# One Trainium2 core: an operand order and placement change in a selective scan between two dense stages

## The chip, the cores and the metric

The kernel runs on one core of one Trainium2 chip. The metric is the device time of one execution in microseconds (us). Before the change three runs took 1060.62, 1064.67 and 1065.10 us, median 1064.67.

## The reference

The input x is (8, 256, 32, 32) in float32: 8 images, 256 channels, N = 1024 tokens. One block is computed, cut here to what matters:

```python
x = x + conv(ln_c(x))                      # ln over channels
t = to_tokens(x)
t = t + ffn(ln_t(t))                       # 8 experts, dense, weights from a thresholded softmax
# conv:
xz = silu(in_proj_w @ x + b)               # 768 x 256
x_ssm, res, gate = split(xz, 3)
xf = silu(depthwise_conv3(x_ssm))
dbc = dbc_w @ xf + b                       # per head: dt, B (8), C (8)
dt = softplus(dbc[:, :, 0])
# x_h, dt, B, C are gathered by perm, an argsort of a Moebius-mapped score (one per head)
h = exp(dt * A) * h + dt * B * x_t         # 8 states, 1024 steps, 2 heads of 128 channels
y_t = C . h + D * x_t
y = y gathered by the inverse of perm
y = y * silu(gate) + res
return silu(out_proj_w @ y + b)
```

## The kernel before, in words

There are three stages, and five engines that each run their own hand-written instruction list; semaphores are the only order between engines. A wait blocks all that stands behind it in that engine's list.

**Stage 1** (`batch(b)`, b = 0 to 7 on every engine) does one image per step: transposes and layer norm, the projection in 6 row blocks (`in_proj`, L1064, three-part products of a high and a low half), the convolution, `dbc` (L1074), and rows by token (`rows_by_tokens`). SyncE stores rows, res and gate to HBM. VectorE ranks the scores in batches 1 to 4 (`ranks`), turns ranks into places in batch 4 (`places`), and GpSimd scatters token numbers to `order_scratch` in batches 5 and 6 (`scatter_order`, 8 indirect DMAs each). SyncE loads the order (`turn`) in its part of batch 7. GpSimd then gathers the first chunks (`gather_rows`).

**Stage 2**, the scan (`body(q)`, q = 0 to 15), takes chunks of 64 tokens, all heads and 4 images in one chunk, so that 8 chunks make 1024 tokens for 4 images, and then the other 4 images follow. A chunk is computed as a kernel matrix and a state. On each engine one `body(q)` works on chunk q and on parts of q - 1, q + 1, q + 2 and q + 3:

- TensorE: `rows_of(q+1)` (transposes of B and C to bank 4), `products(q, ...)`, 8 matmuls C.B, one per state, cycling through banks 1, 2 and 3 (L1185), `times_of(q+1)` (dt summed up to each token, bank 5, L1122 and L1124), `y_of(q-1, 0)` and `y_of(q-1, 1)` (L1194, L1197, banks 6 and 7), `sums_of(q+2)` (L1102, bank 0), `states(q+1)` (L1135) and `columns(q+1)` (L1142).
- ScalarE: `decays` (8 exponentials of 128x512 into `ee`, which is tile `rg`, L921), `rows_high`, `block_decays`, `y_rows` (PSUM to SBUF, L927), `states_by_tile` (8 scaled copies to `hx`, L937), `columns` (L868).
- VectorE: `times_decay(q, s)` (ee times product, L1701), `whole_kernel(q-1)` (last sum, writes `kbd`, L1713), `rows_low`, `distances` (L1652), `weigh` (L1677, L1681), `flatten`, `exponents` (L1638, L1644), `next_states`.
- GpSimd: `add_state(q, s)` for s = 0 to 6 (running sum `ksum` in tile `sm`, L708), `up_to_token(q+2)` (dt times a triangle to `dtri`, L679), `gather_rows(q+3)` (L669).
- SyncE: `spread(q+1)` sends rows to HBM (L449) and reads them back in block form to `cr` and `bl` (L454, L456), which `products(q+1)` needs; then the store of y.

`decays(q, s)` waits until `add_state(q-1, s)` has read the same part of `ee`. `add_state(q, 0)` waits until `whole_kernel(q-1)` has read `ksum`:

```python
if s == 0:
    pool.wait_ge(dskip_ready, 2)
    pool.wait_ge(k_ready.sem, k_ready.at(c.q, 0))
```

**Stage 3** (`step3`, 16 steps of 512 tokens) gathers y, gates it, applies the out projection (L1255), adds the residual, layer norm by token, softmax gate, 8 experts (L1322, the bulk of TensorE's time). A step also prepares the front of the next one. The front of the very first step (gate, out projection, norm, logits) has no step to hide behind: it runs after chunk 15, with y gathered in part during chunks 13 to 15 (`gather_first`), and res and gate of the first half loaded in chunk 14 (`rg0`).

## Time and profile before

| What | Value |
|---|---|
| runs | 1060.62, 1064.67, 1065.10 us |
| the profiled execution | 1064.97 us |
| its span (first to last instruction) | 1063.2 us |
| busy: TensorE, VectorE, ScalarE, GpSimd | 930.4, 771.3, 508.6, 505.9 us |
| granted TensorE clock, mean | 0.917 of full |

The profile is of the one execution of 1064.97 us. The span leaves out 1.8 us before the first and after the last instruction. Busy time is an average over three stages with different limits, so it is read stage by stage.

### The profile page before, as it was taken

What the parts mean: (1) busy time and instruction counts of PE and PEld (TensorE: products, weight loads), DVE (VectorE), ACT (ScalarE), POOL (GpSimd) and SP (SyncE); (2) the same over time, 40 slices, a digit from 0 to 9 for tenths busy, and PEclk for the clock granted to TensorE, in tenths of its full rate; (3) what the DMA queues carried; (4) which work ended last, traced back from release to release, by engine and by line L of the source; (5) the groups of instructions that cost most, each with busy time, mean ns of one, the idle gap of its engine ahead of it and who ended that gap; (6) DMA issues with size and microseconds to landing.
All of it is one profiled execution on the core that took longest, in us unless ns stands there. A gap on an engine that the chain in (4) does not pass through costs nothing.

```text
span 1063.2 us, 15454 instructions
## 1 busy us (share of the span) xinstructions
PE 930.4 (88%) x4658; PEld 718.6 (68%) x4658; DVE 771.3 (73%) x2001; ACT 508.6 (48%) x924; POOL 505.9 (48%) x563
## 2 busy tenths in 40 slices
PE   4999999986687678666499999999999999999997
PEld 3887888874454445444367777777777777877776
DVE  5768887534677778775458787787787877878775
ACT  2777877664666665666223333332333323333330
POOL 2066666775887877788650333313333132330000
PEclk8999999996777887778689999999999999999999
DMA  5335674476254343334331131401314013140001
GB/s 162 119 89 171 190 191 147 116 175 177 76 144 126 98 120 109 117 108 156 126 133 44 33 145 39 147 30 39 138 39 158 21 38 138 39 158 20 20 1 39
DMA packets 63687, 110.05 MB, mean 104 GB/s; under 512 B 18538, under 2 KB 44436, under 8 KB 60564
## 3 DMA queue, kind: packets, MB, share of 16 engines
q1 hardware_dynamic: 56468, 91.41, 27.4%
q0 software_dynamic: 7168, 18.03, 5.9%
q8 instruction: 22, 0.36, 0.1%
q14 instruction: 29, 0.24, 0.1%
HBM read 61.51 MB, written 47.92 MB: 103 GB/s over the span
## 4 chain that ended last, share of the span: by engine, by line
PE 69%; DVE 7%; ACT 7%; issue 5%; POOL 5%; DMA 4%; ACTq 0%; SPq 0%; DVEq 0%; another core or an unknown queue 0%; POOLq 0%
PE bank L1322 31%; PE bank L1064 8%; PE bank L1230 4%; PE bank L1255 4%; PE bank L1185 3%; ACT xf L937 3%; PE bank L1283 2%; PE bank L1074 2%; PE bank L1194 2%; POOL sm L708 2%; PE bank L1197 2%; PE bank L1122 2%; PE bank L1092 2%; DMA score_scratch<-score 1%; PE bank L1267 1%
## 5 line engine op out<-in xcount | busy, mean ns | idle before, releaser
L763 POOL TENSOR_TENSOR ssm<-ssm,rg 128x512 f32<-128x512 f32 x30 | 35.2, 1192 | 269.7 <-DVE ssm L1799 269.7
L751 POOL DMA_INDIRECT xtm<-y_scratch,idxu x120 | 119.2, 993 | 68.6 <-issue 34.2
L1322 PE MATMUL bank<-wexph,xhl 128*128 128x512 f32 x512 | 144.9, 405 | 0.1
L1322 PE MATMUL bank<-wexph,cr 128*128 128x512 f32 x512 | 143.4, 401 | 0.1
L708 POOL TENSOR_TENSOR sm<-sm,rg 128x512 f32<-128x512 f32 x96 | 122.4, 1275 | 30.0 <-DVE rg L1701 20.1
L1701 DVE TENSOR_TENSOR rg<-rg,bank 128x512 f32<-128x512 f32 x128 | 83.2, 681 | 60.6 <-ACT rg L921 39.9
L1322 PEld LDWEIGHTS bank<-wexph,xhl 128*128 128x128 f32 x512 | 93.8, 189 | 23.4 <-DVE xf L1903 2.0
L1322 PEld LDWEIGHTS bank<-wexph,cr 128*128 128x128 f32 x512 | 93.4, 189 | 22.0 <-DVE ysb L1903 1.7
L921 ACT ACTIVATE rg<-dists,aown 128x512 f32<-128x512 f32 x128 | 84.7, 714 | 0.0
L1322 PE MATMUL bank<-wexpl,xhl 128*128 128x512 f32 x256 | 80.6, 396 | 0.0
L1322 PE MATMUL bank<-wexpl,cr 128*128 128x512 f32 x256 | 80.3, 395 | 0.0
L1898 DVE SCALAR_TENSOR_TENSOR ysb<-bank,soft,ysb 128x256 f32<-128x256 f32 x128 | 58.3, 479 | 25.1 <-PE bank L1322 23.0
L1898 DVE SCALAR_TENSOR_TENSOR xf<-bank,soft,xf 128x256 f32<-128x256 f32 x128 | 57.8, 479 | 24.4 <-PE bank L1322 21.5
L1064 PE MATMUL bank<-xhl,winh 128*128 128x512 f32 x192 | 55.0, 408 | 4.0 <-ACT ssm L813 2.0
L1064 PE MATMUL bank<-cr,winh 128*128 128x512 f32 x192 | 55.5, 412 | 3.1 <-ACT ssm L813 2.8
L1322 PEld LDWEIGHTS bank<-wexpl,xhl 128*128 128x128 f32 x256 | 48.3, 189 | 11.6
L1322 PEld LDWEIGHTS bank<-wexpl,cr 128*128 128x128 f32 x256 | 48.1, 188 | 11.3
L1903 DVE SCALAR_TENSOR_TENSOR xf<-bank,soft,xf 128x256 f32<-128x256 f32 x128 | 55.5, 475 | 0.0
L1903 DVE SCALAR_TENSOR_TENSOR ysb<-bank,soft,ysb 128x256 f32<-128x256 f32 x128 | 55.5, 475 | 0.0
L813 ACT ACTIVATE rg<-bank,inb 128x512 f32<-128x512 f32 x64 | 43.5, 686 | 14.6 <-PE bank L1064 13.6
L927 ACT ACTIVATE ysb<-bank 128x512 f32<-128x512 f32 x32 | 19.1, 598 | 64.0 <-PE bank L1197 63.6
L592 POOL TENSOR_TENSOR sp<-euler,sp 128x16 f32<-128x16 f32 x8 | 24.4, 3056 | 48.0 <-DVE sp L1563 47.9
(303 smaller groups left out, 2111.9 us busy)
## 6 DMA issues: line engine op xcount, KB each, us to landing
xin<-in_x SPq DMA_DIRECT2D x16, 1024.0 KB, 5.3
res_gate_scratch<-rg SPq DMA_DIRECT2D x16, 1024.0 KB, 10.9
rg<-res_gate_scratch SPq DMA_DIRECT2D x8, 2048.0 KB
y_scratch<-ysb SPq DMA_DIRECT2D x16, 512.0 KB, 3.6
out<-stage SPq DMA_DIRECT2D x16, 512.0 KB, 2.7
rows_scratch<-xr SPq DMA_DIRECT2D x8, 580.0 KB
rows_scratch<-stage SPq DMA_DIRECT2D x8, 580.0 KB
bc_scratch<-r SPq DMA_DIRECT2D x16, 288.0 KB
```

Of the source, the lines that this page charges most:

```text
L708: pool.tensor_tensor(total, bc(dskip[:, :], 1, ST) if s == 0 else total, new, ALU.add).then_inc(summed.sem, 1)
L751: pool.indirect_dma_start(out=xtm[:, t, h * P:(h + 1) * P], out_offset=None, in_=y_d[b // GB].rearrange("q p s c -> (q p s) c"), in_offset ...
L763: pool.tensor_tensor(z[:, k, :], z[:, k, :], rg[:, k, cols], ALU.add).then_inc(z_ready.sem, 1)
L813: act.activation(dst, bank[2 + hf][:, :], ACT.Silu, bias=inb[:, m:m + 1]).then_inc(mm_used[hf].sem, 1)
L921: act.activation(ee[:, s, :], dist[c.two].rearrange("p t n -> p (t n)"), ACT.Exp, scale=aown[:, s:s + 1]).then_inc(e_ready.sem, 1)
L1064: last = pe.matmul(bank[2 + hf][:, :], w[:, k, m * P:(m + 1) * P], v[:, k, cols], start=(n + k == 0), stop=(n + k == 3))
L1230: last = pe.transpose(dst[:, i * P:(i + 1) * P], src(i), ident[:, :])
L1255: last = pe.matmul(bank[2 + m][:, :], w[:, k, m * P:(m + 1) * P], x_[:, k, :], start=(n + k == 0), stop=(n + k == 3))
L1322: last = pe.matmul(bank[4 + i][:, :], x_[:, k, i * P:(i + 1) * P], w[:, 2 * ep * KC + k:2 * ep * KC + k + KC + 1:KC, :], start=(n + k == 0 ...
L1701: dve.tensor_tensor(ee[:, s, :], ee[:, s, :], bank[BC_BANK + s % 3][:, :], ALU.mult).then_inc(bc_used[s % 3].sem, 1)
L1898: dve.scalar_tensor_tensor(ttm[par][:, i, :], bank[4 + i][:, 0:C], soft[par][:, 2, i, 2 * ep:2 * ep + 1], ttm[par][:, i, :], ALU.mult, ALU ...
L1903: dve.scalar_tensor_tensor(ttm[par][:, i, :], bank[4 + i][:, C:2 * C], soft[par][:, 2, i, 2 * ep + 1:2 * ep + 2], ttm[par][:, i, :], ALU.m ...
```

## The change

- **Order loaded in batch 6**: `places` runs per head, in batches 2 and 4; `scatter_order` runs in quarters in batches 3, 4, 5 and 6; SyncE loads `turn` in batch 6; GpSimd gathers chunks 0 and 1 before the softplus of batch 6 instead of after half of it. The rows of batch 6 are stored by ScalarE's DMA queue. In batch 7 chunk 0's sums, rows and times are placed between the projection's row blocks, its exponents ahead of the second convolution. `cr[0]` is zeroed at the head of batch 7; `cr[1]` is zeroed inside `body(0)` (one memset of 128x4096).
- **Chunk reordered**: `ksum` has two buffers, so `add_state(q, 0)` waits for `whole_kernel(q-2)` only. ScalarE runs all its decays, then `states_by_tile`, then both `y_rows`. TensorE runs one product ahead of `rows_of`. VectorE runs `exponents` ahead of `times_decay(q, 6)`.
- **Operands in PSUM**: `argx` lives in bank 0, `args` is computed from the sums in bank 0, and the last product (s = 7) is written back to its bank 2, from where `whole_kernel` reads it. So `products(q, 1)`, the next user of bank 2, waits for `whole_kernel(q-1)`.
- **dt times triangle on ScalarE**: 8 scaled copies of 128x64 per chunk from chunk 2 on, in place of one GpSimd op of 128x512.
- **Last stage's first step in chunks 14 and 15**: y's first half is gathered in chunks 9 to 12, the second in chunks 13 to 15; gate, out projection and residual of step 0 stand inside chunks 14 and 15, in banks 5 and 4.

```diff
-        argx = sb("argx", [P, 2, ST, HEADS * S])
+        argx = bank[0][:, SUB:SUB + 2 * P].rearrange("p (i t x) -> p i t x", i=2, t=ST)
-        ksum = sm[:, 0:4, :].rearrange("p s n -> p (s n)")
+        ksum = [sm[:, 4 * i:4 * i + 4, :].rearrange("p s n -> p (s n)") for i in range(2)]
...
-                if b == NB - 1:
-                    sync.wait_ge(order_stored, 16 * HEADS * NT)
+                if b == NB - 2:
                     for h in range(HEADS):
+                        sync.wait_ge(order_stored[h], 16 * NT)
...
-                if b == NB - 3:
-                    scatter_order(0)
-                if b == NB - 2:
-                    scatter_order(1)
+                if NB - 5 <= b < NB - 2:
+                    scatter_order(*divmod(b - NB + 5, 2))
...
-                    pool.wait_ge(k_ready.sem, k_ready.at(c.q, 0))
+                    if c.q:
+                        pool.wait_ge(k_ready.sem, k_ready.at(c.q - 1, 0))
...
                 for s in range(S - 1):
+                    if q == CHUNKS - 2 and s in (S - 3, S - 2):
+                        first_z(s - S + 3)
                     add_state(c, s)
-                if q + 2 < CHUNKS:
-                    up_to_token(Chunk(q + 2))
...
+                if NT < q <= NT + TPH:
+                    gather_first(0, [(q - NT - 1, h) for h in range(HEADS)])
+                if q in SECOND_Y:
...
+            def up_to_token(c):
+
+                act.wait_ge(xr_ready[c.row].sem, xr_ready[c.row].at(c.turn4, 32))
+                act.wait_ge(b_full.sem, b_full.at(c.q, 0))
+                for t in range(ST):
+                    last = act.activation(dtri[:, t, :], tri[:, :], ACT.Copy, scale=dt_of(c)[:, t:t + 1])
+                last.then_inc(dtri_ready.sem, 1)
...
                 if q:
-                    y_rows(Chunk(q - 1), 0)
+                    decays(c, 2, S)
+                    states_by_tile(c)
+                    for h in range(HEADS):
+                        y_rows(Chunk(q - 1), h)
...
+                if q + 2 < CHUNKS:
+                    up_to_token(Chunk(q + 2))
                 if q + 1 < CHUNKS:
                     columns(Chunk(q + 1))
...
+                    if s == 1:
+                        pe.wait_ge(k_ready.sem, k_ready.at(c.q, 0))
                     pe.wait_ge(bc_used[s % 3].sem, bc_used[s % 3].at(c.q, s // 3))
...
+                products(c, 0, 1)
                 if q + 1 < CHUNKS:
                     rows_of(Chunk(q + 1))
-                products(c, 0, 3)
+                products(c, 1, 3)
                 if q + 1 < CHUNKS:
                     times_of(Chunk(q + 1))
+                if q == CHUNKS - 1:
+                    out_proj(0, FRONT_BANKS)
                 products(c, 3, 4)
+                if q == CHUNKS - 2:
+                    first_y_by_channels(0)
...
-                dve.tensor_tensor(args[:, :, :, :], bc(cs[:, :, :], 3, HEADS * S),
+                dve.tensor_tensor(args[:, :, :, :], bc(sums.rearrange("p (i t) -> p i t", i=2), 3, HEADS * S),
...
+                else:
+                    dve.tensor_tensor(bank[BC_BANK + s % 3][:, :], ee[:, s, :], bank[BC_BANK + s % 3][:, :],
+                                      ALU.mult).then_inc(last_product.sem, 1)
...
+                if q == CHUNKS - 1:
+                    low_z(0)
...
                 if q + 2 < CHUNKS:
                     flatten(Chunk(q + 2))
+                    exponents(Chunk(q + 2))
                 times_decay(c, 6)
-                if q + 2 < CHUNKS:
-                    exponents(Chunk(q + 2))
                 times_decay(c, 7)
+                if q == CHUNKS - 1:
+                    residual(0, 0)
```

How the instructions stand, at the three places that the prediction speaks of. First TensorE in the middle of the scan, from one chunk's `rows_of` to the next; before:

```order
L1113 MATMUL bank<-ident,bct 64x128 x2
L1115 MATMUL bank<-ends,args 128x1
L1185 MATMUL bank<-xhl,bl 128x512 x3
L1122 MATMUL bank<-dtri,same 128x512
L1124 MATMUL bank<-bigr,identr 128x512
L1185 MATMUL bank<-xhl,bl 128x512
L1194 MATMUL bank<-xf,cwt 128x512
L1197 MATMUL bank<-xr,kbd 128x128 x4
```

and now:

```order
L1265 MATMUL bank<-xhl,bl 128x512
L1188 MATMUL bank<-ident,bct 64x128 x2
L1190 MATMUL bank<-ends,args 128x1
L1265 MATMUL bank<-xhl,bl 128x512 x2
L1197 MATMUL bank<-dtri,same 128x512
L1199 MATMUL bank<-bigr,identr 128x512
L1265 MATMUL bank<-xhl,bl 128x512
L1274 MATMUL bank<-xf,cwt 128x512
L1277 MATMUL bank<-xtm,kbd 128x128 x4
```

One product (L1265, before L1185) has moved ahead of the transposes; the other two of the three stand where they were, now behind the new wait for `whole_kernel`. Second, ScalarE's whole chunk now (before, `y_rows` of ysb stood between the decays of rg, and there was no dtri):

```order
L884 ACTIVATE cwt<-bank 128x128
L946 ACTIVATE rg<-dists,aown 128x512 x2
L865 ACTIVATE dec<-bank 128x1
L879 ACTIVATE bank<-args 128x256
L946 ACTIVATE rg<-dists,aown 128x512 x6
L970 ACTIVATE xf<-hs,own_rows 128x128 x8
L960 ACTIVATE ysb<-bank 128x512 x2
L954 ACTIVATE dtri<-tri,xr 128x64 x8
```

Six decays now run in a row, and the 8 new copies stand last, ahead of the next chunk's columns. Third, VectorE in chunk 15, from the whole kernel of chunk 14 to that of chunk 15:

```order
L1820 TENSOR_TENSOR kbd<-sm,bank 64x8x64 x2
L1885 TENSOR_TENSOR xhl<-ssm,xhl 128x512 x2
L1805 TENSOR_TENSOR rg<-rg,bank 128x512 x6
L1808 TENSOR_TENSOR bank<-rg,bank 128x512
L1894 TENSOR_TENSOR ssm<-ssm,xin 128x512 x2
L1900 BN_STATS bst<-xf 128x6 x4
L1904 BN_AGGR mv<-bst 128x2 x4
L1906 TENSOR_SCALAR mv<-mv 128x4
L1820 TENSOR_TENSOR kbd<-sm,bank 64x8x64 x2
```

The low half of z (L1885), the residual (L1894) and the statistics of step 0 now stand ahead of the last whole kernel; they all came after it before.

## Rows read from the trace of the kernel before

**Rows 1.** Windows by stage: us, busy time (count) per engine, PEclk, DMA share, GB/s

```profile
294.40:476.90 182.50, 133.76 (x669) 88.68 (x668) 140.72 (x285) 115.60 (x298) 145.05 (x122) 0.78 0.43 120
...
538.00:1063.20 525.20, 511.19 (x2487) 398.87 (x2485) 408.13 (x1110) 170.93 (x261) 138.59 (x135) 1.00 0.20 71
```

**Rows 2.** Timeline of TensorE, the first experts of the last stage

```profile
538.05 1.71 PE L1322 MATMUL bank<-wexph,xhl 128*128 128x512 f32 x4
```

**Rows 3.** Timeline of GpSimd: its first op behind the last sum of chunks 1 and 13

```profile
294.42 1.06 POOL L679 TENSOR_TENSOR dtri<-xr,tri 128x512 f32<-128x512 f32 x1
...
476.85 1.24 POOL L679 TENSOR_TENSOR dtri<-xr,tri 128x512 f32<-128x512 f32 x1
```

**Rows 4.** The chain of waits, scan, one chunk: start us, us, what

```profile
370.48 1.49 PE bank L1185 x3
371.97 1.71 PE bank L1122 x2
...
374.53 1.44 PE bank L1194 x2
...
378.18 0.91 PE bank L1197 x8
...
379.66 2.43 ACT xf L937 x8
382.09 0.62 ACT rg L921
```

**Rows 5.** Timeline of VectorE, scan; the first row is from the time ahead of chunk 0

```profile
239.06 0.43 DVE L1644 TENSOR_TENSOR args<-cs,acol 128x256 f32<-128x256 f32 x1
...
387.31 0.69 DVE L1701 TENSOR_TENSOR rg<-rg,bank 128x512 f32<-128x512 f32 x1 [0.90 <-PE bank L1185]
387.91 1.40 DVE L1713 TENSOR_TENSOR kbd<-sm,rg 64x512 f32<-64x512 f32 x2
...
390.00 0.67 DVE L1652 TENSOR_TENSOR dists<-bank,cs 128x512 f32<-128x512 f32 x1
...
398.64 1.51 DVE L1644 TENSOR_TENSOR args<-cs,acol 128x256 f32<-128x256 f32 x1
```

**Rows 6.** Windows of 1 us, TensorE alone: us, busy (count), PEclk, DMA share, GB/s

```profile
383.00:384.00 1.00, 0.34 (x8) 0.50 0.57 229
...
389.00:390.00 1.00, 1.00 (x4) 0.89 0.62 121
```

**Rows 7.** Timeline of GpSimd, scan: start us, us, then line, operation, operands, count

```profile
274.52 1.24 POOL L679 TENSOR_TENSOR dtri<-xr,tri 128x512 f32<-128x512 f32 x1
...
282.31 1.06 POOL L669 DMA_INDIRECT xr<-rows_scratch,turn  x1 [0.28 <-issue]
...
391.34 6.95 POOL L708 TENSOR_TENSOR sm<-sm,rg 128x512 f32<-128x512 f32 x5 [0.58 <-DVE rg L1701]
```

**Rows 8.** Timelines of TensorE, SyncE's queue and VectorE, ahead of chunk 0

```profile
234.84 1.08 PE L1064 MATMUL bank<-cr,winh 128*128 128x512 f32 x4
...
238.67 3.74 PE L1074 MATMUL bank<-wdbc,xf 128*128 128x34 f32 x32
...
260.74 1.65 PE L1185 MATMUL bank<-xhl,bl 128*128 128x512 f32 x3 [9.56 <-DMA bl<-bc_scratch]
...
246.01 1.08 SPq L449 DMA_DIRECT2D bc_scratch<-r  x1
...
251.46 3.47 DVE L1767 MEMSET cr<- 128x4096 f32 x1 [0.80 <-issue]
```

**Rows 9.** SyncE's queue and TensorE, chunk 15: from the store of its rows to its products

```profile
482.33 0.45 SPq L449 DMA_DIRECT2D bc_scratch<-r  x1
...
491.59 2.44 PE L1185 MATMUL bank<-cr,bl 128*128 128x512 f32 x4 [3.01 <-DMA bl<-bc_scratch]
```

**Rows 10.** Timeline of TensorE, chunk 15, at the lower clock: the matmuls of one y_of

```profile
494.60 2.04 PE L1194 MATMUL bank<-xf,cwt 128*128 128x512 f32 x2 [0.57 <-issue]
496.43 1.91 PE L1197 MATMUL bank<-xr,kbd 128*128 128x128 f32 x8
```

More of the change, by code:

```diff
@@ L364, in metaformer @@
         WEXP_PARTS = 4
+        FRONT_BANKS = (5, 4)
         def row_bank(b, f):
@@ L1361, in step3 @@
                     y_by_channels(b + 1, hf, True)
[L1363 removed]
+            chunks(body)
+            t_by_tokens(0, FRONT_BANKS)
             for i in range(2):
                 y_of(Chunk(CHUNKS - 1), i)
+            normalised_by_channels(0, xn0, FRONT_BANKS)
+            logits(0, 0)
             pe.wait_ge(wexp_low, WEXP_PARTS)
[L1367 to L1370 removed]
+            for h in range(HEADS):
+                pe.wait_ge(y2_used[h].sem, y2_used[h].at(CHUNKS, 0))
             experts(0, 0, 0, 1)
@@ L1608, in batch @@
                     dbc_in(b - 1)
+                if not ahead:
+                    zero_rows(0, NB - 1)
                 convolve(b, 0)
@@ L1948, in _ @@
             own.settle()
-            own = Steps(dve, dve3, 0)
-            low_z(0)
-            residual(0, 0)
+            low_part(0, 0, FRONT_BANKS)
+            softmax_in(front, 0, 0)
+            front.end()
             next_rows(0)
-            normalise(own, 0, 0)
-            low_part(0, 0)
-            softmax_in(own, 0, 0)
-            own.end()
             with dve.Fori(0, NB - 1) as b:
```

310 lines of the change are left out of this document (187 added, 123 removed).

## The prediction

> **What bounds the kernel now.** I read the windows by stage first. In the last stage TensorE is busy 511.19 of 525.20 us at full clock [rows 1], and its loop is not touched: from the first experts at 538.05 [rows 2] to the end at 1063.2 are 525.1 us that stay. In the middle of the scan no engine is full: of 182.50 us GpSimd is busy 145.05, VectorE 140.72, TensorE 133.76, ScalarE 115.60, and TensorE's clock averages 0.78 [rows 1]. So the scan is bound by a ring of waits. GpSimd ends its last sum of chunk 1 at about 294.4 and that of chunk 13 at about 476.85 [rows 3]: 12 chunks in 182.4 us, 15.2 each. The chain of waits then shows the ring [rows 4]: three products 1.49, the two matmuls of `times_of` (L1122, 1.71, and L1124, about 0.43), two `y_of` (the first 1.44 + 0.89, the second 0.86 + 0.91), ScalarE's copy of y, the 8 state copies 2.43, one decay 0.62, its product on VectorE, then `states`, `columns` and back to the products. The state copies stand behind both copies of y on ScalarE only by the order of its list.
>
> **The chunk, new ring.** The change takes that ring apart and makes another. Product 1 of chunk q now waits for `whole_kernel(q-1)`, because that reads bank 2. Behind this product on TensorE stand product 2, `times_of(q+1)` and both `y_of`; `distances(q+1)` waits for `times_of` and stands ahead of `times_decay(q, 1)` on VectorE, and `add_state(q, 1)` waits for that. Counted from the end of the last sum of chunk q-1:
> - `whole_kernel` 1.40 [rows 5];
> - products 1 and 2: two of three that took 1.49 [rows 4], 1.0;
> - `times_of` 1.71 + 0.43 [rows 4], 2.15. The three ran at half clock in the rows: it was 0.50 at 383 us and rose at 389 us [rows 6];
> - `distances` 0.60 and `times_decay(q, 1)` 0.69 [rows 5], 1.3;
> - six sums, s = 1 to 6: five took 6.95 [rows 7], so one comes every 1.42; 8.4;
> - hand-overs between engines, 0.1.
>
> That is 14.35 us. The four gathers' issues and sum 0 lie inside it: gathers about 2.3 [rows 7] and 1.42 end at 3.7, before sum 1 may start at 5.95. The GpSimd triangle of 1.24 [rows 7] is gone, but it is off this ring; its worth is only that GpSimd alone would now need 7 x 1.42 + 2.3 = 12.2.
>
> There is a second ring through ScalarE, because its list now ends with y, triangle, columns, decay 0: 1.40 + 1.0 + 2.15 as above, product 3 0.43, first `y_of` 1.44 + 0.89, products 4 and 5 0.5, second `y_of` 0.86 + 0.91 [rows 4], copy of y 0.6, the 8 triangle copies, columns 0.3, decay 0.7, product 0.69 [rows 5], hand-overs 0.6. Without the triangle 12.5. **The triangle on ScalarE** has no row before. The nearest is the 8 state copies of twice the width, 2.43 [rows 4]; half of it, 1.2, is the floor, if the width were all. I take 2.0, near the upper end, because the one copy of half the work need not take half the time. The ring is then 14.5, between 13.7 and 14.9. Two rings of the same length disturb each other, so I take 14.5 for a chunk: 0.7 less than now, 8.4 us over 12 chunks.
>
> **Operands in PSUM.** `args` takes 1.51 in the scan and took 0.43 ahead of it, when GpSimd was not summing [rows 5]; it is the same instruction, and the two differ by a wait of up to one GpSimd sum. With its first operand in PSUM I give it 0.43 to 0.5; likewise `weigh`. Both stand off the new rings, where VectorE idles for `distances` or for `sums_of`, so I cost them at nothing; without this cover they would bring up to 2 us a chunk. The same row has a price for another part of the change: `low_z` and `residual` of step 0 read two SBUF operands as `args` did, and move to where GpSimd sums. I put one such wait, 1.1 (1.51 - 0.43), on each pair in the tail below. The Trainium skill (GPSIMD Engine Reference, Specifications) says that GpSimd's SBUF interfaces are shared with VectorE and contended by instructions with two SBUF inputs. It speaks against the moved pairs; if it did not hold for them, the sum would be 2 us lower.
>
> **The start.** `rows_of(0)` moves ahead of one row block (234.84 to 238.67 without sums and gap, 2.9) and of `dbc` (3.6 of 3.74) [rows 8], less about 0.5 of table loading and waiting that moves with it: 6.0 us. So SyncE's store of chunk 0's rows goes from 246.01 to 240.0. To the products it took 14.7 then, with other stores under way [rows 8]; undisturbed, chunk 15 shows 9.26 [rows 9]. Now it meets the 1 MB res store and the rows store that moves to ScalarE's queue, so I keep 14.7: products at 254.7 (249 to 259). The earlier order makes this possible, since the gathers of chunks 0 and 1 no longer wait for it; SyncE in return holds back its rows and res stores of batch 6 by some 4 us, which only ScalarE's third row block of batch 7 waits for, about at the edge.
>
> But the memset of `cr[1]`, 3.47 [rows 8], was hidden in the wait for chunk 0, and now stands in chunk 0 behind `distances(1)`, about 5.1 after the products. It ends at 8.6; SyncE's spread of chunk 1 waits for it, and 9.26 later, at 17.9, product (1, 0) starts. Its decay product ends at 19.1, `whole_kernel(0)` at 20.5. GpSimd ends chunk 0's sums at 17.7, has softplus (from 275.8 to 282.3, 6.1 without gaps) and gathers, 8.4 more [rows 7], so sum (1, 1) starts at 27.6 and the last ends at 36.1. That is 290.8 against 294.4. **The start gives 3.6**, not 6.0.
>
> **First gathers in chunks 9 to 12**: two more issues each, 2.5 us on GpSimd. Gathers and sum 0 then end at 2.3 + 2.5 + 1.4 = 6.2 or a little later, against 5.95: 0.4 a chunk, a loss of 1.6.
>
> **The tail**, from the last sum of chunk 13. Before, the first experts came at 538.05, 61.2 us later [rows 2, 3]. Now, on the same prices: sums of chunk 14 start as in any chunk, with three more gathers hidden; `first_z` twice stretches GpSimd's list by 2 x 1.45, so its last sum ends at 14.35 + 2.9 = 17.3. Meanwhile ScalarE waits for the second z (15.9), copies it, does columns and decay 0 of chunk 15: product 0 on VectorE ends at 18.3, `whole_kernel(14)` at 19.7, `low_z` at 21.5 with its wait. `out_proj`, 12 matmuls, starts there at half clock, 4.5; product 3 at 26.4; first `y_of`, products 4 and 5, second `y_of`, products 6 and 7: 31.7. VectorE ends at 33.0, the residual at 35.2. Transposes 1.8, copy 0.6, statistics and their aggregate 2.1: 39.2 (a little overlaps). `whole_kernel(15)` 1.4, normalise 1.7: 42.3. The last `y_of` pair keeps TensorE to 44.5; transposes, high part, low part, logits 5.0: experts at 49.5. **The tail gives 61.2 - 49.5 = 11.7**. I bound it by 7 (all TensorE work there at half clock) and 16 (no waits between VectorE and GpSimd, full clock).
>
> **Sum:** 3.6 + 8.4 - 1.6 + 11.7 = 22.1 us off the profiled execution's 1064.97: 1042.9. That execution stands 0.3 above the median of the three runs, so it needs no correction.
>
> **The rivals.**
> - *The clock stays up.* TensorE's idle time ahead of product 1 is some 2.4 us in my walk, so the clock may not fall there. The rows show it at half level, 1.2 GHz, at 383 us, when only a third of the microsecond was busy, and back near 2.4 GHz at 389 us, after some 5 us of work [rows 6]; matmuls cost half when it is up. Then products and `times_of` take 1.6 instead of 3.15, the first ring is 12.9 and the second under 13; GpSimd is near its own 12.2, and the four chunks with first gathers cost 14.9. Over 12 chunks 8 x 2.2 + 4 x 0.3 = 18.8, the start 3.6, the tail up to 14: 36 off, 1029. The Trainium skill (TensorE: Matmul & The Clock Gate, What's actually happening) has the clock set by how busy the engine has recently been. By that rule a shorter stop speaks for this rival; the trace's 0.78 over a scan that is busy 73% of its time speaks against.
> - *The clock rises late.* If it stays at half until the first `y_of` is over, that costs 3.4 (494.60 to 498.0, two parts [rows 10]) instead of 2.33, and the second ring is 15.5: 12 x 0.3 lost, tail 9, start 3.6, gathers hidden: about 9 off, 1056.
> - *Slower: ScalarE's list closes the ring at half clock.* The mechanism is the second ring with TensorE at half clock throughout, since it now works in one burst behind `whole_kernel`: both `y_of` at 3.4 and products 4 and 5 at 0.9, the triangle at 2.4, which gives 18.0. Then 12 x 2.8 = 33.6 are lost, and start and tail give 3.6 + 7: 23 slower, 1088. It decides from a chunk of about 16.1 on. For it speaks that everything on TensorE now waits for one event; against it that its work in a chunk is as much as before, and the clock did rise each time.
> - *The edit does not free the start*: the stores that move onto each other cost what the earlier rows gain. Then 3.6 falls away or turns to -3: 1047 to 1050. It goes with any of the others and is inside the range.
>
> **How the numbers follow.** Forecast (chunk 14.0 to 15.0, with either start) 0.58; clock stays up 0.18; clock rises late 0.17; slower ring 0.07. A measurement of this kernel tells about 0.5%, 5.3 us, from no change. Faster by more: forecast, clock up, and most of the late clock, 0.88. Same 0.06, from the late clock with a bad start. Slower 0.06. The range takes in the clock rival and the late one: 1026 to 1058.
>
> **What would show it.** In the new profile: last sums of chunks 1 and 13 some 176 us apart; TensorE idle ahead of products 1 and 2, released by VectorE's whole kernel; `args` and `weigh` without their waits; 8 triangle copies in about 2 us; first experts near 516 us; the stage behind them 525 us. I am wrong in the main step if chunks take under 13.8 or over 15.2, in the tail if it is not 47 to 53 us, in the start if chunk 1's last sum is not at 287 to 295.

## The result and the profile after

The changed kernel took 1046.21 us (median of 4 runs, 1044.32 to 1047.31), the kernel before 1063.87 beside it (1060.62 to 1065.10): a ratio of 0.984, 95% interval 0.981 to 0.986, so 1.6% faster. The forecast was 1042.9 us, faster, with a range of 1026 to 1058.

| What | Before | After |
|---|---|---|
| the profiled execution | 1064.97 us | 1047.31 us |
| its span | 1063.2 us | 1044.4 us |
| last sum of chunk 1 ends | 294.4 | 290.20 |
| last sum of chunk 13 ends | 476.9 | 465.84 |
| first experts start | 538.05 | 514.34 |
| from there to the end | 525.1 | 530.1 |

Windows by stage of the kernel after (us, busy time and count of TensorE, its weight loads, VectorE, ScalarE, GpSimd, then granted clock, DMA share, GB/s), for [rows 1]. They are: from the first product to the last sum of chunk 1, 12 chunks of the scan, the tail, the last stage, and the part of it up to the out projection of its step 1:

```profile
255.30:290.20 34.90, 22.17 (x113) 14.63 (x113) 23.50 (x48) 27.53 (x78) 25.95 (x36) 0.80 0.35 102
290.20:465.84 175.64, 128.91 (x672) 84.98 (x672) 125.47 (x288) 137.38 (x394) 137.58 (x116) 0.83 0.47 133
465.84:514.30 48.46, 30.85 (x137) 20.46 (x138) 27.82 (x56) 24.91 (x51) 28.26 (x24) 0.79 0.35 121
514.30:1044.40 530.10, 511.82 (x2487) 400.16 (x2486) 409.17 (x1114) 171.11 (x261) 146.71 (x142) 0.99 0.20 71
514.34:532.04 17.70, 11.17 (x58) 8.60 (x56) 9.68 (x30) 4.79 (x7) 11.08 (x11) 0.94 0.18 41
```

The last row is new. In the kernel before, the same work, from the first experts to that out projection, took 12.42 us with GpSimd busy 5.51:

```profile
538.05:550.47 12.42, 11.80 (x57) 9.13 (x56) 8.78 (x26) 5.02 (x7) 5.51 (x6) 0.95 0.24 71
```

The chain of waits of the kernel after, from the last sum of chunk 1 on (start, us, what), for [rows 4]:

```profile
290.22 0.68 DVE kbd L1820
...
291.68 1.22 PE bank L1265 x2
292.90 1.71 PE bank L1197 x2
294.61 0.26 PE bank L1199
...
295.51 0.69 DVE rg L1805
296.27 1.30 POOL sm L713
...
304.69 0.68 DVE kbd L1820
...
306.91 6.05 DMA bc_scratch<-r
...
315.82 2.90 DMA bl<-bc_scratch
318.77 0.81 PE bank L1265
```

The first part is the ring of the forecast: whole kernel (L1820), products 1 and 2 (L1265), `times_of` (L1197, L1199), a decay product (L1805), six sums (L713), whole kernel again after 14.47 us. The second part is one that the forecast did not have. In the next chunk the chain leaves through SyncE: the store of the rows, the 8 loads, and products that wait for `bl`. The chunks are not all alike: from last sum to last sum, chunks 2 to 13 took 14.45, 14.61, 15.59, 14.60, 13.09, 15.49, 14.31, 14.56, 14.96, 14.64, 14.67 and 14.67 us.

TensorE in windows of 1 us in one chunk (busy time, count, clock, DMA share, GB/s), for [rows 6]. It stands still from 376.7 to 379.5 (the full clock is still granted then), drops to half clock as it restarts, and is back near full in the window from 383:

```profile
378.00:379.00 1.00, 0.00 (x0) 1.00 0.00 0
...
380.00:381.00 1.00, 1.00 (x3) 0.50 0.72 237
...
383.00:384.00 1.00, 1.00 (x4) 0.85 0.76 309
```

In chunk 6 the clock did not fall, though TensorE had waited 2.19 us for the whole kernel. The granted clock was 1.00 in each microsecond from 346 to 362, products 1 and 2 took 0.74 instead of 1.22, and the six sums began 4.7 us behind the last sum instead of 6.1. This chunk is the short one, 13.09. GpSimd's timeline:

```profile
354.17 8.37 POOL L713 TENSOR_TENSOR sm<-sm,rg 128x512 f32<-128x512 f32 x6 [1.04 <-DVE rg L1805]
```

VectorE (first five rows) and ScalarE (last two) of the kernel after, timeline (start, us, operation, idle before and its releaser), for [rows 5]:

```profile
357.18 1.26 DVE L1734 COPY bct<-xin 128x128 f32<-128x128 f32 x1
...
388.19 0.41 DVE L1746 TENSOR_TENSOR args<-bank,acol 128x256 f32<-128x256 f32 x1
...
392.37 1.40 DVE L1820 TENSOR_TENSOR kbd<-sm,bank 64x512 f32<-64x512 f32 x2 [0.66 <-POOL sm L713]
...
483.43 2.55 DVE L1885 TENSOR_TENSOR xhl<-ssm,xhl 128x512 fp32r<-128x512 f32 x2
...
496.22 2.35 DVE L1894 TENSOR_TENSOR ssm<-ssm,xin 128x512 f32<-128x512 f32 x2
```

```profile
381.73 2.45 ACT L970 ACTIVATE xf<-hs,own_rows 128x128 f32<-128x128 f32 x8
...
387.76 2.01 ACT L954 ACTIVATE dtri<-tri,xr 128x64 f32<-128x64 f32 x8
```

`args` has lost its wait, 0.41 for 1.51. But a part of the wait has only moved: the copy `bct`, SBUF to SBUF, took 0.28 in the kernel before and takes 1.03 to 1.28 now. (The first row is from another chunk than the second.) The 8 triangle copies take 2.01 where the 8 state copies of twice the width take 2.45.

Last, the start of the last stage in the kernel after, GpSimd, VectorE and TensorE:

```profile
518.52 0.94 POOL L769 DMA_INDIRECT xtm<-y_scratch,idxu  x1 [16.62 <-DVE idxu L1871]
...
528.21 2.31 POOL L781 TENSOR_TENSOR ssm<-ssm,rg 128x512 f32<-128x512 f32 x2
```

```profile
530.17 1.73 DVE L1885 TENSOR_TENSOR xhl<-ssm,xhl 128x512 fp32r<-128x512 f32 x2 [5.05 <-ACT xhl L998]
```

```profile
532.04 2.07 PE L1342 MATMUL bank<-xhl,wouth 128*128 128x512 f32 x4 [6.00 <-DVE xhl L1885]
```

GpSimd had stood idle 16.62 us for the row numbers of the next gathers (`next_rows`, L1871), which VectorE now writes behind the first half of the softmax of step 0, at 517.5. Eight gathers' issues, 9.7 us, then stand ahead of the gate times y (L781) that the out projection of step 1 needs, and TensorE waits 6.00 us and restarts at the lower clock (2.07 for four matmuls that took 1.19 before).

### The profile page after: what moved, and what is told of

It is laid out like the page before. It is cut to its first block, busy times and chain, and to the rows that moved or that the text cites. A ratio compares the mean times of both kernels' runs of the same rounds, so it can differ in the third digit from the quotient of the medians.

```text
span 1044.4 us, 15615 instructions
## 1 busy us (share of the span) xinstructions
PE 922.5 (88%) x4658; PEld 714.8 (68%) x4658; DVE 754.0 (72%) x2003; ACT 534.7 (51%) x1036; POOL 485.3 (46%) x549
## 3 DMA queue, kind: packets, MB, share of 16 engines
q10 hardware_dynamic: 2080, 1.19, 0.7%
## 4 chain that ended last, share of the span: by engine, by line
PE 62%; POOL 15%; DVE 6%; DMA 6%; issue 6%; ACT 3%; SPq 1%; ACTq 0%; POOLq 0%; DVEq 0%
PE bank L1409 34%; POOL sm L713 9%; PE bank L1137 6%; PE bank L1342 5%; PE bank L1314 4%; PE bank L1370 2%; PE bank L1147 2%; PE bank L1265 2%; PE bank L1354 1%; DMA score_scratch<-score 1%; DVE kbd L1820 1%; DMA bc_scratch<-r 1%; DMA res_gate_scratch<-rg 1%; DMA bl<-bc_scratch 1%; PE bank L1197 1%
## 5 line engine op out<-in xcount | busy, mean ns | idle before, releaser
L781 POOL TENSOR_TENSOR ssm<-ssm,rg 128x512 f32<-128x512 f32 x30 | 35.1, 1192 | 262.0 <-DVE ssm L1879 262.0
L769 POOL DMA_INDIRECT xtm<-y_scratch,idxu x112 | 111.6, 996 | 78.4 <-DVE idxu L1871 47.5
L713 POOL TENSOR_TENSOR sm<-sm,rg 128x512 f32<-128x512 f32 x96 | 122.6, 1277 | 42.5 <-DVE rg L1805 30.6
L1805 DVE TENSOR_TENSOR rg<-rg,bank 128x512 f32<-128x512 f32 x112 | 72.4, 680 | 25.6 <-PE bank L1265 17.1
L946 ACT ACTIVATE rg<-dists,aown 128x512 f32<-128x512 f32 x128 | 81.8, 721 | 0.0
L1265 PE MATMUL bank<-cr,bl 128*128 128x512 f32 x64 | 29.2, 521 | 28.3 <-DVE kbd L1820 21.6
L1265 PE MATMUL bank<-xhl,bl 128*128 128x512 f32 x64 | 28.9, 516 | 28.5 <-DVE kbd L1820 17.9
```

Source lines behind the costliest of these rows:

```text
L713: pool.tensor_tensor(total, bc(dskip[:, :], 1, ST) if s == 0 else total, new, ALU.add).then_inc(summed.sem, 1)
L769: pool.indirect_dma_start(out=xtm[:, t, h * P:(h + 1) * P], out_offset=None, in_=y_d[b // GB].rearrange("q p s c -> (q p s) c"), in_offset ...
L946: act.activation(ee[:, s, :], dist[c.two].rearrange("p t n -> p (t n)"), ACT.Exp, scale=aown[:, s:s + 1]).then_inc(e_ready.sem, 1)
L1265: pe.matmul(bank[BC_BANK + s % 3][:, :], bl[c.two][:, s, :], cr[c.two][:, s, :], start=True, stop=True).then_inc(bc_full[s % 3].sem, 1)
L1805: dve.tensor_tensor(ee[:, s, :], ee[:, s, :], bank[BC_BANK + s % 3][:, :], ALU.mult).then_inc(bc_used[s % 3].sem, 1)
```

## Experiments

Each ratio is to the kernel before, run beside it on the same chip, with its 95% interval. The chips differ (one for experiments 1, 2, 6 and 7, one for 3, 4, 5 and 8, one for 9 to 11), so medians of different experiments are compared best by their ratios; 0.001 is 1.1 us. "Mean" is the length of a chunk in the one profiled execution, over chunks 2 to 9, from the last sum of chunk 1 to that of chunk 9. It is 15.13 us in the kernel before and 14.59 in the changed one. Experiments 1 and 9 leave these chunks' code alone and have 14.57 and 14.45, so a difference of 0.2 is not clear of noise. All are edits of the changed kernel, and the diffs are cut to their main lines.

**1. Row numbers ahead of the low part.**

```diff
             own.settle()
+            next_rows(0)
             low_part(0, 0, FRONT_BANKS)
             softmax_in(front, 0, 0)
             front.end()
-            next_rows(0)
```

> The changed kernel, with next_rows(0) moved from behind softmax_in(0) to ahead of low_part(0), that is some 12 us earlier in VectorE's list. Theory: GpSimd's 8 gathers for step 2 wait for the new indices until 518.5 and hold back the sum z of step 1, so TensorE idles 6.0 us before out_proj of step 1 and then runs it at the lower clock (5.25 instead of 2.84). The gathers then start at about 511 and end before the z sum is wanted: 5 to 8 us faster, 1038 to 1041, and the idle time before that out_proj under 1 us. Rival: the last stage lost its 5 us for another reason (the load of rg late, or banks), then no change.

Measured: 1040.59 us (1039.20 to 1042.88), ratio 0.978 [0.974, 0.982]. GpSimd's first gather and TensorE's out projection of step 1, in its timelines:

```profile
514.86 0.94 POOL L769 DMA_INDIRECT xtm<-y_scratch,idxu  x1 [8.65 <-PE bank L1314]
```

```profile
529.01 1.19 PE L1342 MATMUL bank<-xhl,wouth 128*128 128x512 f32 x4 [0.53 <-DVE xhl L1885]
```

The first experts were at 517.21, so the out projection comes 11.8 behind them instead of 17.7, at full clock. From the first experts to the end of the span (1039.1) are 521.9 us, where the kernel before took 525.1 and the changed one 530.1. The 5 us that the last stage lost are this one placement: without it the stage is 8.2 shorter, 5.9 up to the out projection and 2.3 from there on, with its matmuls no longer at the lower clock. In the median the gain is 5.6 us; the two intervals meet at 0.981 to 0.982, so it is the profile that makes the case.

**2. The last product back in SBUF**, so that product 1 no longer waits for the whole kernel. In return decay 7 of the next chunk, which overwrites it, waits for the whole kernel instead of for the last product.

```diff
-                    if s == 1:
-                        pe.wait_ge(k_ready.sem, k_ready.at(c.q, 0))
...
-                    dve.tensor_tensor(bank[BC_BANK + s % 3][:, :], ee[:, s, :], bank[BC_BANK + s % 3][:, :],
-                                      ALU.mult).then_inc(last_product.sem, 1)
+                    dve.tensor_tensor(ee[:, s, :], ee[:, s, :], bank[BC_BANK + s % 3][:, :], ALU.mult).then_inc(
+                        bc_used[s % 3].sem, 1)
```

> The changed kernel (1046.2 us), but the last product (s = 7) is written back to ee in SBUF as before the change, so products(q, 1) no longer waits for whole_kernel. Theory (the ring of the prediction: whole kernel 1.40, products and times_of 3.15, distances and decay product 1.3, six sums 8.4): the ring loses its second link, GpSimd then binds with 7 sums and the gathers' issues, 12.2 to 12.4 a chunk in chunks 2 to 9, 14.7 in chunks 10 to 13 as now; if the second ring, through ScalarE's list, is then the longest, 13 to 14. Expected 1046.2 - 8 x (1 to 2.2), 1029 to 1039, and GpSimd's sums without the idle time of 2 to 3.5 us behind sum 0. Rival: whole_kernel with both operands in SBUF collides with GpSimd's sums and takes 2.5 instead of 1.40, which gives back a part: 1038 to 1046. Second rival: the ring through ScalarE already binds by itself, no change, 1044 to 1048.

Measured: 1042.03 us (1038.63 to 1043.34), ratio 0.979 [0.975, 0.983], mean 13.90. The interval overlaps with that of the changed kernel; the mean per chunk, 0.69 shorter, is beyond what unchanged chunks vary by. The time fell by less than expected. The chain of waits gives one reason:

```profile
320.29 1.65 DVE kbd L1812
321.97 0.49 DVE r L1761 x3
...
322.77 3.16 DMA bc_scratch<-r
...
328.76 2.92 DMA bl<-bc_scratch
...
348.42 5.01 DMA bc_scratch<-r
```

The chain now runs through SyncE: whole kernel, `rows_low` (L1761) behind it, store, loads, products. Opening one ring uncovered the other. The second reason is the first rival, and the time lies in its range too: with both operands in SBUF again, the whole kernel took 2.36 to 2.64 us instead of 1.40 in the four cases where GpSimd was at sum 0 beside it (the row of 1.65 is half of one; 0.70 is usual). These are the whole kernels ahead of chunks 3, 4, 7 and 8, which took 14.58 to 15.54, while chunks 2, 6 and 9 took 12.5 to 12.6. In the changed kernel it took 1.40 each time, and in experiment 6 too, where it has its operand in PSUM and sum 0 runs beside it (at 392.82 and 393.34, for one). Which part of a long chunk is the late spread and which the collision was not run apart.

**3. Experiment 2, and `rows_low` ahead of the whole kernel on VectorE.**

```diff
+                if q + 1 < CHUNKS:
+                    rows_low(Chunk(q + 1))
                 if q:
                     whole_kernel(Chunk(q - 1))
...
                 if q + 1 < CHUNKS:
-                    rows_low(Chunk(q + 1))
                     distances(Chunk(q + 1))
```

> The run with the last product back in SBUF, and on top of it VectorE writes rows_low of the next chunk ahead of the whole kernel instead of behind it. Theory (once product 1 no longer waits for the whole kernel, the bound is SyncE's spread: VectorE's rows_low behind the whole kernel's 1.4 us, store 3.2, loads 2.3 to issue and 2.9 to land, products, and back): the spread starts up to 1.5 to 1.9 us sooner, chunks 1 to 9 come every 12.4 to 13.2 us instead of 13.9, chunks 10 to 13 stay at about 15 (GpSimd), and the run takes 1029 to 1037 against 1042.0 without the move. Rival (the spread waits for something else, such as the rows of bank 4 or the buffer of cr, or the ring goes through ScalarE): the mean stays at 13.7 to 14.1 and the time within 3 us of 1042.

Measured: 1035.07 us (1034.05 to 1037.88), ratio 0.974 [0.969, 0.979], mean 12.98, as the theory had it; clear of the changed kernel, while against experiment 2 only the mean is clear. GpSimd's timeline shows what bounds a chunk there:

```profile
356.98 1.41 POOL L671 DMA_INDIRECT xtm<-rows_scratch,turn  x1
...
359.66 1.30 POOL L711 TENSOR_TENSOR sm<-dskip,rg 128x512 f32<-128x512 f32 x1
361.11 8.35 POOL L711 TENSOR_TENSOR sm<-sm,rg 128x512 f32<-128x512 f32 x6
369.60 1.42 POOL L671 DMA_INDIRECT xr<-rows_scratch,turn  x1
```

From 356.98 to 369.60 are 12.62 us of gathers and sums without a gap: GpSimd alone. The windows from 290 to 395 us, first of experiment 2, then of this one, show the clock with it:

```profile
290.00:395.00 105.00, 82.11 (x420) 53.73 (x419) 82.13 (x184) 85.58 (x244) 82.98 (x68) 0.82 0.48 135
```

```profile
290.00:395.00 105.00, 79.55 (x456) 52.44 (x455) 86.57 (x198) 94.76 (x274) 89.61 (x74) 0.92 0.51 143
```

456 matmuls take less time than 420 did, as the clock is 0.92 for 0.82. This is the rival "the clock stays up" with its chunk of under 13. It takes both edits: in experiment 2 TensorE no longer stops for the whole kernel, but it stops for the spread. Whether the clock makes the chunk short or the short chunk keeps the clock up is not separated.

**4. The changed kernel with the same move alone**, the last product left in PSUM (the diff is that of experiment 3).

> The changed kernel with the same single move (rows_low of the next chunk ahead of the whole kernel), the last product left in PSUM. Theory (the predicted ring through whole kernel, product 1, times_of, distances, sum 1 to sum 6 binds most chunks, and SyncE's spread only some): rows_low of about 0.6 us now stands in the predicted ring, since it delays the whole kernel, while the spread comes sooner; chunks 1 to 9 mean 14.3 to 15.0 instead of 14.6, time 1042 to 1050. Rival (the spread binds in the changed kernel too, and the ring of the prediction only looked right by its size): the mean falls to 13.5 or less and the time to 1033 to 1038.

Measured: 1049.63 us (1047.68 to 1051.39), ratio 0.986 [0.981, 0.992], mean 15.03. Its chain of waits:

```profile
360.58 1.95 ACT dtri L954 x8
...
364.54 0.17 ACT r L871
364.73 0.49 DVE r L1765 x3
...
366.13 0.70 DVE kbd L1820
366.88 1.22 PE bank L1265 x2
```

The move that gave some 5 us by the ratios there (7 by the medians, from two chips) gives nothing here: 0.986 against 0.984, with intervals that overlap, and a mean of 15.03 against 14.59, just above the theory's 15.0 and clearly longer. `rows_low` waits for ScalarE's high rows (L871), these stand behind y, triangle and decay 0, and the whole kernel, and through it product 1, now waits for all of it: the ring through ScalarE, closed by the wait on product 1. So the wait on product 1 decides what the order of `rows_low` is worth.

**5. The triangle back on GpSimd**, everything else as changed.

```diff
                     add_state(c, s)
+                if q + 2 < CHUNKS:
+                    up_to_token(Chunk(q + 2))
...
-                if q + 2 < CHUNKS:
-                    up_to_token(Chunk(q + 2))
                 if q + 1 < CHUNKS:
                     columns(Chunk(q + 1))
```

> The changed kernel with dt times the triangle as one GpSimd op of 128x512 (1.24 us) behind the last sum again, nothing of it on ScalarE. Theory (the first ring binds and GpSimd idles 2 to 3.5 us behind sum 0 in chunks 1 to 9, ScalarE's list is the second ring of nearly the same length): chunks 1 to 9 keep 14.2 to 14.7 us, chunks 10 to 13, where GpSimd is full, take 15.9 instead of 14.7, and the time is 1046 to 1052. Rival (ScalarE's 1.6 to 1.9 us of triangle copies stand in the binding ring in every chunk): chunks 1 to 9 fall to 13.5 or less and the time to 1038 to 1043.

Measured: 1049.30 us (1044.38 to 1051.93), ratio 0.986 [0.980, 0.992], mean 14.54; chunks 10 to 13 took 15.70 each, where chunks 11 to 13 of the changed kernel take 14.64 to 14.67. Its chain of waits is the predicted ring from whole kernel to whole kernel, 14.63 us:

```profile
349.43 0.68 DVE kbd L1820
...
350.89 1.22 PE bank L1265 x2
...
364.06 0.68 DVE kbd L1820
```

The triangle's new place is worth 1.0 us in the chunks that GpSimd fills and nothing in the others. On ScalarE it costs nothing there either: the second ring of the prediction loses its 2.0 us here, and the mean stays. So that ring does not bind in the changed kernel. In the time the difference, by ratio some 2 us, is within the intervals.

**6. ScalarE's old order**, in chunks 1 to 15 (the expectation has 1 to 13): the copies of y between the decays, the state copies behind them.

```diff
-                    decays(c, 2, S)
-                    states_by_tile(c)
-                    for h in range(HEADS):
-                        y_rows(Chunk(q - 1), h)
+                    decays(c, 2, 4)
+                    y_rows(Chunk(q - 1), 0)
+                    decays(c, 4, 6)
+                    y_rows(Chunk(q - 1), 1)
+                    states_by_tile(c)
+                    decays(c, 6, S)
```

> The changed kernel with ScalarE's list of chunks 1 to 13 in the old order: both copies of y between the decays, then the state copies, then decays 6 and 7, then the 8 triangle copies and the columns. Theory: the second y_of ends about 10 us after the last sum; copy 0.6, state copies 2.4, two decays 1.3, triangle 1.7, columns 0.3, decay 0 0.7, its product 0.7 make a chunk of 17.6 to 18: 30 to 42 us slower than the changed kernel, 1076 to 1088, slower than the kernel before. So the triangle on ScalarE pays only with the new order. Rival: the list's order does not matter as long as ScalarE is busy under 80%: 1044 to 1049.

Measured: 1076.07 us (1075.73 to 1081.08), ratio 1.013 [1.009, 1.017], mean 17.16. A little less than the theory's 17.6 per chunk, but its mechanism stands in the chain. The span is 29.6 us longer: 29.9 more in chunks 2 to 13 and 2.7 more in the tail, less 3.0 elsewhere.

```profile
402.92 2.18 ACT xf L970 x8
...
405.26 1.32 ACT rg L946 x2
406.58 1.54 ACT dtri L954 x7
...
408.65 0.62 ACT rg L946
```

State copies, two decays, triangle and columns in a row stand between y and the next decay 0. The new order of ScalarE's list is what makes the rest of the change pay: without it the kernel is slower than before. How much of this is the triangle's, which stands in this ring with 1.9 us, was not run apart.

**7. `argx` and the operand of `args` back in SBUF.**

```diff
-        argx = bank[0][:, SUB:SUB + 2 * P].rearrange("p (i t x) -> p i t x", i=2, t=ST)
+        argx = sb("argx", [P, 2, ST, HEADS * S])
...
-                dve.tensor_tensor(args[:, :, :, :], bc(sums.rearrange("p (i t) -> p i t", i=2), 3, HEADS * S),
+                dve.tensor_tensor(args[:, :, :, :], bc(cs[:, :, :], 3, HEADS * S),
```

> The changed kernel with argx in SBUF and args computed from the SBUF copy cs, as before the change; the last product stays in PSUM. Prediction: both stand off the rings, costed at nothing: 1044 to 1049. Rival: args again takes 1.5 and weigh 0.9 more, and states(q+1), columns and decay 0 of the next chunk stand behind args, so the second ring grows by about 1.1 and binds: 5 to 12 us slower, 1051 to 1058.

Measured: 1048.56 us (1047.30 to 1051.51), ratio 0.987 [0.983, 0.990], mean 14.53. The waits come back,

```profile
355.79 1.24 DVE L1781 TENSOR_TENSOR bwx<-xr,argx 64x64 f32<-64x64 f32 x1
...
358.41 0.28 DVE L1734 COPY bct<-xin 128x128 f32<-128x128 f32 x1
...
358.75 1.32 DVE L1747 TENSOR_TENSOR args<-cs,acol 128x256 f32<-128x256 f32 x1
```

some 1.9 us a chunk (0.23 and 0.41 were measured with PSUM operands), while the copy `bct` between them is back at 0.28 for 1.26. In sum VectorE is busy 1.1 us a chunk more (92.8 us for 83.8 in chunks 2 to 9), and the chunks get no longer on average. The waits are covered, as costed; and of the 1.9 that PSUM operands take away, VectorE gets 1.1.

**8. The memset of `cr[1]` ahead of chunk 0's body.**

```diff
             next_states(first)
+            zero_rows(1, NB)
...
-                if q == 0:
-                    zero_rows(1, NB)
```

> The changed kernel with the memset of the second cr buffer (128x4096, 3.47 us) back ahead of chunk 0's body. Theory (the prediction's: in chunk 0 the memset stands between distances(1) and rows_low(1), and chunk 1's spread waits for it): products of chunk 1 come up to 3.5 us sooner, the last sum of chunk 1 1.5 to 3.5 us sooner than 290.2, and the time is 1042.5 to 1045. Rival (GpSimd's softplus and gathers of 8.4 us bind chunk 1's sums anyway): the last sum of chunk 1 moves by under 1 us and the time stays within 1.5 us of 1046.2.

Measured: 1044.43 us (1041.73 to 1049.44), ratio 0.981 [0.976, 0.986], which overlaps that of the changed kernel. The last sum of chunk 1 came at 292.9, later than 290.2, but so did the first product, at 259.0 for 255.3, with nothing edited ahead of it. The time lies in the theory's range, the last sum of chunk 1 in nobody's. The rival's mechanism holds from chunk 0 to chunk 1: their last sums are 17.80 apart, and were 17.76, and between them GpSimd's list is full in both, with softplus and gathers from 272.4 to 280.4 in the changed kernel, then seven sums. In chunk 0 itself the memset stands in the chain in either place (3.47 us at 260.18 here), since ahead of the body it holds back the first decay product instead of the second. Counted from the first product, the last sum of chunk 1 came after 33.9 us, for 34.9 in the changed kernel and 36.2 in experiment 1, which starts alike. So some 1 us may be gained there; the times don't tell it.

**9. The last quarter of the scatter behind the softplus of batch 5.**

```diff
-                if b == NB - 2:
-                    scatter_order(1, 1)
                 if b:
                     softplus_back(b - 1)
+                if b == NB - 2:
+                    scatter_order(1, 1)
```

> The changed kernel with the last quarter of the scatter behind the softplus of batch 5 instead of ahead of it, in GpSimd's part of batch 6. Theory (SyncE's stores of batch 6 are held back by the order, and through them ScalarE's third row block of batch 7; a later scatter holds them longer): the res store goes out 1 to 3 us later than 217.5, and the last sum of chunk 1 and the end come 0 to 4 us later: 1046 to 1050. Rival (softplus is what batch 7 waits for, and the order has slack): 1 to 3 us sooner, 1043 to 1045.

Measured: 1047.47 us (1046.06 to 1050.95), ratio 0.989 [0.986, 0.992]. In SyncE's queue the order load and the first store of res came later than in the changed kernel, 216.22 and 218.45 for 213.76 and 217.54; the last sum of chunk 1 ended at 291.5 for 290.2. It has the sign of the theory, but a single execution's start moves by more than that: in experiment 1, which touches nothing ahead of it, the order load came at 216.01, the store of res at 219.69 and the last sum of chunk 1 at 292.9. The ratio is higher than the changed kernel's (the intervals just meet), but that one ran on another chip, and the profiled span, 1044.3, is the same. Not settled.

**10 and 11. The best of them together**: experiments 1 and 3 in one kernel, without and with the early memset of experiment 8.

> Three moves together on the changed kernel: the last product back in SBUF (no wait ahead of product 1), rows_low of the next chunk ahead of the whole kernel, and next_rows(0) ahead of low_part(0). Theory (the three faults lie in different places, the first two in the scan's chunks and the third behind the first experts, so they add): 1035.1 of the first two, less the 5 to 6 us that the third gave alone: 1028 to 1031, with the out projection of step 1 some 11.8 us behind the first experts. Rival (the scan's end, which is bound by TensorE's and GpSimd's own lists, takes back what the chunks give, or the third move gains only where the tail is late): 1033 to 1036.

> The same three moves and the memset of the second cr buffer ahead of chunk 0. Theory (that memset is not what chunk 1 waits for, as the run with it alone showed: 17.8 us from the last sum of chunk 0 to that of chunk 1, with it and without): within 2 us of the kernel without this fourth move. Rival (in the quicker scan chunk 1's spread is what binds, so the memset counts now): 2 to 3.5 us faster.

Measured: 1023.55 us (1021.60 to 1026.05), ratio 0.966 [0.964, 0.968], and 1023.41 us (1019.60 to 1029.16), ratio 0.966 [0.963, 0.969]. The second differs from the first by 0.1, as its theory had it: the memset's place does not show here either. The first lies 4.5 us below the low end of what was expected; the kernel before was itself 2.0 us quicker on this chip than beside experiment 3 (1060.05 for 1062.08), so some 2.5 of it are left. In the profiles, the time from the first experts to the end fell from 529.5 in experiment 3 to 522.0, so `next_rows` is worth 7.5 there, near the 8.2 of experiment 1's profile; the first experts came 4.5 sooner (499.10 for 503.59), of which 3.2 in chunks 2 to 9, with a mean of 12.58 for 12.98, though no edit touches them. Experiment 3's profile has two chunks of 14.0 and 14.7 among its 12.6s, the first of these two has none before chunk 10, and the second (mean 12.84) has one of 14.7. The profiles show what goes with it. Ahead of each of these three long chunks, and of no other up to chunk 13, VectorE's whole kernel came late, ran beside GpSimd's sum 0, and took 2.82, 2.44 and 2.81 us instead of 1.40; in the first kernel's profile it never did. Both of the 14.7 are chunk 4, and there the lateness follows a store of chunk rows that took 5.4 us instead of 3.1. What makes that store long is open.

## Why the prediction was right, and where it was not

The working went by times from the start, so it can be held against the profile step by step.

- **Start: right.** First product 254.7 forecast, 255.31 measured; last sum of chunk 1 290.8 and 290.2. That GpSimd's softplus, gathers and seven sums set this end holds, and so does the memset on the path of chunk 0 (experiment 8). Such closeness is partly luck: in the profiles of the experiments the first product came between 252.3 and 259.0.
- **The chunk: right, with one ring missing.** 12 chunks were to take 175.6 us and took 175.64. The new ring was put at 14.35 and is 14.47 in the changed kernel and 14.63 in experiment 5; of its terms only the two products were dearer, 1.22 for 1.0. The second ring through ScalarE exists (experiments 4 and 6), but it does not bind here, as experiment 5 takes 2.0 us out of it and the chunk stays. Not foreseen was the third, through SyncE's spread: `rows_low` behind the whole kernel, store, loads, products. It stood in the chain of the changed kernel in some chunks (15.59 in chunk 4), and the sum came out right partly since "two rings of the same length disturb each other" left 0.15 for what was in truth a third one, and since the short chunk 6, at full clock, pays for the long chunk 4. The sum over 12 chunks is steadier than the single chunks: 175.5 and 174.5 in experiments 1 and 9, with the same code.
- **First gathers in chunks 9 to 12: right in cause, too dear by 1.** Gathers and sum 0 were to end at 6.2, and six sums of 8.4 behind that make a chunk of 14.6 in which GpSimd is full. That is what chunks 11 to 13 show, 14.64 to 14.67. But the walk added its 0.4 to the 14.5 of a chunk, and not to the 14.35 of the ring that it was worked out from, so it had 14.9. The four chunks took 58.9 where 59.6 were forecast, 0.6 more than four mean ones, for 1.6.
- **Triangle: right.** 2.0 was taken between 1.2 and 2.4, 2.01 measured in the row shown. Half the width saved only 0.44 of 2.45 over 8 copies.
- **PSUM operands: right as to cost, wrong in one place.** `args` and `weigh` are hidden (experiment 7); that a copy would take over 0.9 of their wait was not seen, and is hidden too. But for the last product the choice has a price that was counted as a term and never weighed: the wait it brings is 0.7 us a chunk by itself, and keeps another 0.9 shut in (experiments 2 and 3). It also buys something that was not counted: the whole kernel, with one operand in PSUM, did not wait for a sum of GpSimd in any row read (1.40 beside sum 0 in experiment 6), and that wait costs 1.0 to 1.4 us where it happens. The 0.7 and 0.9 are what is left after that.
- **Tail: right in its sum, by two errors that nearly cancel.** 49.5 forecast, 48.5 measured. The last whole kernel was to end at 40.6 and ended at 37.7: chunk 14 was 2.0 quicker than walked. The last `y_of` pair then took 6.65, at half clock nearly throughout, where the walk had 3.9. The price of 1.1 for each moved pair was right: `low_z` took 2.55 and the residual 2.35 beside GpSimd's sums. In the kernel before, beside nothing but gathers' issues, they took 1.29 and 1.45 (the first is shown):

```profile
516.73 1.29 DVE L1805 TENSOR_TENSOR xhl<-ssm,xhl 128x512 fp32r<-128x512 f32 x2
```

The Trainium skill (GPSIMD Engine Reference, Specifications) has GpSimd's SBUF interfaces shared with VectorE and contended by instructions with two SBUF inputs. Those rows agree, and so do those of experiment 7.

- **Last stage: the step that failed.** "From the first experts at 538.05 to the end at 1063.2 are 525.1 us that stay", as "its loop is not touched". It took 530.1. The loop was not touched, but what its first step finds was: `next_rows(0)` had moved behind the softmax, and behind it GpSimd's gathers. Before, these gathers' issues ran from 528.78 to 538.5, so they were over as the first experts began. Experiment 1 gives the 5 us back. Against the profiled execution, 4.4 us above the forecast, the account is 5.0 from here and 1.1 more outside the span, less 1.6 by which the experts came sooner.

Of the rivals, "the clock stays up" came in one chunk: chunk 6, with 13.09 us near the 12.9 that it was given. In others TensorE stops ahead of product 1 (for 2.8 us in the one shown, 376.7 to 379.5) and restarts at 0.50. Not each such stop lowers the clock, so which way a chunk goes is not foretold by its length alone: 2.2 us left it up in chunk 6, and 2.6 us (356.0 to 358.6) in experiment 3. The Trainium skill (TensorE: Matmul & The Clock Gate, What's actually happening) has the clock set by how busy the engine has recently been. The fall behind the stop agrees; but over a longer stretch the busy share does not order the clocks, as experiment 2 has 0.82 while TensorE is busy 78% of 105 us, and experiment 3 has 0.92 with 76%. The rival that was slower than before did not come either, but experiment 6 shows that its mechanism is real and one edit away.

## What to carry to other kernels

When a result is kept in a buffer that another engine will refill, the price is the refill's wait, and all that stands behind it in its list; here a faster operand for one instruction made TensorE wait in every chunk. Its gain can lie elsewhere than in the length of that instruction, in that it keeps clear of another engine's. A ring that you find by walking the engines is not the only one: walk each DMA's store and loads as a ring of its own, from the instruction that releases the store, and expect it to appear as soon as the first is opened. And when work is moved forward out of a stage that "is not touched", look at what its first instructions wait for, the row numbers of a gather included, since an engine with an in-order list turns a late small input into a late large output.

## What was not expected of the hardware

The first gather's issue behind the sums took 1.41 us in most chunks of experiments 2 and 3 but 0.96 in the changed kernel (L673, at 407.05 and 422.01); most other issues take 0.94 to 0.96 in all. It starts as VectorE's whole kernel does, which reads two SBUF operands there (`sm` and `rg`) and one in the changed kernel (`sm` and the bank). Chunks 11 to 13, which GpSimd fills, are 15.06 to 15.08 long in experiment 2 for 14.64 to 14.67. So the PSUM place of the last product does buy 0.4 us where GpSimd binds, while it costs more where it does not. The kernel before has the same where an issue happens to fall beside a VectorE operation of two SBUF operands: 1.42 at 310.55, with the whole kernel from 310.47 to 311.87, and 1.38 at 524.79, beside the residual; its other issues in the scan mostly take 0.94 to 0.99. The whole kernel itself waits for a sum in the same way (experiments 2, 3 and 11). That the operands are the cause is inferred from these rows; no run changed them alone.

The copy `bct` has one SBUF operand and an SBUF result, and still took 1.26 for 0.28 beside GpSimd's sums in the changed kernel. In experiment 7 and in the kernel before it comes just as one of these sums ends (358.4 and 395.5) and takes 0.28. So a wait that is taken from one instruction can fall on the next that reads and writes SBUF alone.

The store of chunk rows to HBM (`bc_scratch`) stands in the chains with 3.16, 5.01 and 6.05 us for the same 18 KB. From its issue to that of the first load, it took 3.1 at 343.85, 355.80 and 368.42 in experiment 3, where it is issued ahead of the gathers, and 4.3 to 4.6 at 380.28, 394.59, 409.16 and 424.12 in the changed kernel, 2 us behind the first of them. What lengthens it was not tried.
